# DLRM tower on one core: most of z0's fields move between the k's of the last step's G2

## The chip, the cores and the metric

The kernel runs on one core of one Trainium2 chip. The metric is the device time of one execution in microseconds (us); of the runs the median is given. The engines are TensorE (PE, with its weight loads shown as PEld), VectorE (DVE), ScalarE (ACT), GpSimd (POOL) and SyncE (SP), and each works through its own queue of instructions; semaphores order them among one another.

## The reference

512 samples look up 32 rows of 64 numbers each. Three layers of a compressed interaction network follow, and then a small tower of matrix products:

```
e = stack([tbl_f[ids[:, f]] for f in 32])                     # 512 x 32 x 64
nxt = einsum('bjk,bzk,ojz->bok', h, e, W) + b[:, None]        # three layers, 128 outputs
h, o = nxt[:, :64], nxt[:, 64:]                               # the last layer keeps all of nxt as o
z = sum over k of [o0 | o1 | o2]                              # 512 x 256
h = relu([z | dense_ctx] @ W_top1 + b_top1)
h = relu(h @ W_top2 + b_top2)
y = h @ W_top3
```

All numbers are fp32. Only the sum over k of each layer's o is wanted. Called z0, z1 and z2, these three sums can be had from Gram matrices: z0 is a product of W0 with G0 = e eᵀ of each sample, z1 one of W1 with G1 = h0 eᵀ, z2 one of W2 with G2.

## The kernel before

**Steps.** The samples are taken 16 at a time, in 32 steps. In each step PE computes H (`h_matmuls`, line 383, from products that DVE makes), transposes it (L394), forms G0 (`g0_matmuls`, L403), T (`t_matmuls`, L424 and L427) and G2 (`g2_matmuls`, L440 to L464). T holds, among others, G1 of the step's samples. ACT and DVE copy T from PSUM into T_sb; SP then sends G1 into X and G0 into `kept` by DMA. In the loop G2 of a step stands after H of the next one, and the last step's G2 stands behind the loop.

**Shapes on TensorE.** The 128 by 128 array is used in pieces. A matmul's piece is named in the profile by rows*columns: H and z0 use eight pieces of 32*64, G2, G0 and T four of 64*64, z1 two of 128*64, the transposes of H two of 64*128, z2 and the tower the whole array. An fp32 matmul shows as two passes in the trace, each with its weight load.

**G2.** It runs over k from 0 to 15. Each k has one matmul at L440, one at L444 and two at L450, and from k = 4 on two at L464; the four pieces of the array get 256 columns each.

**The end.** Behind the loop (L505 to L573) PE does z2 of the first half of the samples, six fields of z0, G2 of the last step, five fields of z0, z1, the last five fields of z0, z2 of the second half, and the tower. A field y of z0 is eight matmuls of 128 columns, one for each piece, four into psT and four into psX; all 16 fields add up in the same PSUM banks. The order is written out by hand; there is no scheduler. Before its first matmul G2 waits for the copies of T, and lets SP go on (`t_stored`) to send the last G1; z1 waits for that (`g1_sent`). ACT copies, in this order: G2 (L624), the first half of z2 (L666), z1 (L673), z0's high half (L677), the second half of z2 (L666). DVE adds the two parts of G2 (L810) and the halves of z0 (L840). z2's second half waits for that sum of G2 (`g2_added`), and the tower's first stage (L556) for z0 and z1 (`za_evac`).

Of the kernel before, what the change touches and what calls it, by code (L numbers as in the profile page):

```python
# [19 lines left out]
STEPS = B // SMP  # L20
# [3 lines left out]
HF = NF // 2  # L24
# [24 lines left out]
NTH = [W_SEQUENCE[:k].count(w) for k, w in enumerate(W_SEQUENCE)]  # L49
NSMALL = 9  # L50
NLATE = 6
Z0_CHUNKS = ((0, 6), (6, 11), (11, HF))

T_BY_ACT, T_BY_DVE = (0, 2, 4, 6, 7), (1, 3, 5)
NA, ND = len(T_BY_ACT), len(T_BY_DVE)
# [6 lines left out]
def dlrm_tower(nc, dense_ctx, ids, tables, W_top1, b_top1, W_top2, b_top2, W_top3,  # L62
               W0, b0, W1, b1, W2, b2, y_out):
    ctx = ExitStack()
    with ctx:
# [6 lines left out]
        def sem(name):  # L72
            return ctx.enter_context(nc.semaphore(name))
# [89 lines left out]
        z0_ready, z1_ready, z2_ready = sem("z0_ready"), sem("z1_ready"), sem("z2_ready")  # L163
# [110 lines left out]
        def _(pe):  # L274
# [153 lines left out]
                                  tile_position=(C * h, C))  # L428
                    last.then_inc(t_ready, 1)

            def g2_matmuls(n, first, last_k):
                if first == 0:
                    pe.wait_ge(t_by_act, NA * (n + 1))
                    pe.wait_ge(t_by_dve, ND * (n + 1))
                    pe.sem_inc(t_stored, 1)
                low, high = slice(0, C), slice(C, P)
                cross = T_slots[low, :, :].rearrange("p (v c) s -> p v c s", v=2)[:, :, 0:L_COLS, :]
                for k in range(first, last_k):
                    start, stop = k == 0, k == HF - 1
                    mm(psT[low, 0, 0:HF * SMP], W1d[low, HF + k, :],  # L440
                       cross.rearrange("p v (z y) s -> p v z y s", y=HF)[:, :, :, k, :],
                       start=start, stop=stop, tile_position=(0, 0))
                    row = D_COLS * (k // 8) + HF * (k % 8)
                    mm(psT[high, 0, 0:HF * SMP], W1d[low, k, :], T_flat[low, SMP * row:SMP * (row + HF)],  # L444
                       start=start, stop=stop, tile_position=(0, C))
                    a, i = k // 4, k % 4
                    for v in range(2):
                        out = psT[C * v:C * v + C, 1, 0:HF * SMP]
                        row = D_COLS * v + ROW * i + SHIFT[a]
                        last = mm(out[:, SMP * 4 * a:], W1d[high, HF * v + k, :],  # L450
                                  T_flat[high, SMP * (row + 4 * a):SMP * (row + HF)],
                                  start=start, stop=stop and not a, tile_position=(C, C * v), skip_group_check=True)
                    if a:
                        for v in range(2):
                            out = psT[C * v:C * v + C, 1, 0:HF * SMP]
                            at = D_COLS * v + k
                            rows = T_flat[high, SMP * D_COLS * v:SMP * D_COLS * (v + 1)]\
                                .rearrange("p (i w s) -> p i w s", i=4, s=SMP)
                            if a == 1:
                                moving = rows[:, :, k, :]  # L460
                            else:
                                moving = rows[:, :, k:k + SHIFT[1] * (a - 1) + 1:SHIFT[1], :]\
                                    .rearrange("p i b s -> p b i s")
                            last = mm(out[:, 0:SMP * 4 * a], W1d[high, HF * v + k, :], moving,  # L464
                                      start=False, stop=stop, tile_position=(C, C * v), skip_group_check=True)
                if last_k == HF:
                    last.then_inc(g2_ready, 1)

# [9 lines left out]
            def step(n, lookups):  # L478
                pe.wait_ge(t_by_dve, ND * (n + 1))
                h_matmuls(n + 1)  # L480
                g2_matmuls(n, 0, 4)
                h_transposes(n + 1)
                if lookups:
                    pe.wait_ge(rows_in, 16 * FQ * (n + 1))
                    x_transposes(E_q, psX[:, 3, :])
                g2_matmuls(n, 4, HF)
                if lookups:
                    for evac in x_evac:
                        pe.wait_ge(evac, QUARTERS + n + 1)
                pe.wait_ge(px_ready, n + 2)  # L490
                pe.wait_ge(ht_ready, n + 2)
                tower_in_turn(n + 1)
# [24 lines left out]
                              start=False, stop=(j == 3))  # L517
                last.then_inc(z2_ready, 1)

            def z0(chunk):  # L520
                for y in range(*Z0_CHUNKS[chunk]):
                    for j in range(4):
                        r = slice(Q * j, Q * j + Q)
                        for v in range(2):
                            last = mm(Z0_BANKS[j // 2][C * v:C * v + C, j % 2].rearrange("p (n c) -> p n c", c=4),  # L525
                                      W0z[r, HF * v + y, :], kept[r, :, :, 1 + HF * v + y],
                                      start=(y == 0), stop=(y == HF - 1), tile_position=(Q * j, C * v))
                return last
# [2 lines left out]
            z2(0)  # L531
            pe.wait_ge(t_by_act, NA * STEPS)
            pe.wait_ge(g0_kept, 16 * 4 * STEPS + 1)
            z0(0)
            g2_matmuls(STEPS - 1, 0, HF)
            z0(1)
            pe.wait_ge(g1_sent, 32 * STEPS)
            for y in range(HF):
                for half in range(2):
                    n0 = STEPS // 2 * half  # L540
                    last = mm(psX[C * half:C * half + C, 2, 0:HALF_B].rearrange("p (n s) -> p n s", s=SMP),  # L541
                              W1h[:, y, :], G1_all[:, n0:n0 + STEPS // 2, y, :],
                              start=(y == 0), stop=(y == HF - 1), tile_position=(0, C * half))
            last.then_inc(z1_ready, 1)
            z0(2).then_inc(z0_ready, 1)
            pe.wait_ge(g2_added, 2 + STEPS)
            pe.wait_ge(zb_evac, 1)
            z2(1)
# [14 lines left out]
            for a in range(4):  # L563
                pe.wait_ge(h1_evac, a + 1)
                for m in range(2):
                    last = mm(psX[:, m, :], Wt2[:, a, P * m:P * m + P], h1[:, a, :],
                              start=(a == 0), stop=(a == 3))
                    if a == 3:
                        last.then_inc(h2_ready, 1)
            for a in range(2):  # L570
                pe.wait_ge(h2_evac, a + 1)
                last = mm(psX[0:1, 2, :], Wt3[:, a:a + 1], h2[:, a, :], start=(a == 0), stop=(a == 1))
# [298 lines left out]
```

## Time and profile before

| what | us |
|---|---|
| median of 3 runs | 657.89 (657.76 to 658.94) |
| the profiled execution's own time | 655.34 |
| its span, first to last instruction | 653.6 |
| PE busy in the span | 624.6 |
| DVE, ACT, POOL busy | 483.5, 214.2, 127.9 |
| from z0's first matmul to z2's second half | 603.98 to 626.48 |

The profile shows one execution. Its rows give starts and durations in us, the matmuls' ends are modelled, and several matmuls are in the array at the same time, so that a busy share near 100% says only that PE always had one under way.

### The profile page before, as it was taken

The page shows a single profiled execution, that of the slowest core. Times are in us where ns is not written, and L with a number is a line of the kernel's source. Part 1 is how long each engine was busy: PE and PEld are TensorE (multiplying, and loading weights), DVE is VectorE, ACT ScalarE, POOL GpSimd, SP SyncE. Part 2 cuts the span into 40 slices and gives each one's busy share as a digit, 9 for nine tenths or more (in the row PEclk, how much of TensorE's full clock was granted, in tenths as well). Part 3 has the DMA queues.
Part 4 walks back from the last instruction along what each step waited for, and adds up shares of the span by engine and source line. Part 5 has one row for each costly group of instructions (what it writes and reads, how often), then busy time and mean ns, then how long its engine had stood idle before and what let it go on. Part 6 is the DMA issues. An engine that isn't in the chain of part 4 may idle for free.

```text
span 653.6 us, 32258 instructions
## 1 busy us (share of the span) xinstructions
PE 624.6 (96%) x14488; PEld 516.1 (79%) x14488; DVE 483.5 (74%) x497; ACT 214.2 (33%) x354; POOL 127.9 (20%) x137
## 2 busy tenths in 40 slices
PE   6657999999999999999999999999999999999998
PEld 6645788888888888878888888888888888888773
DVE  4548888888888888878888888888888888841000
ACT  2314333344433433433233333332333333332012
POOL 7764434354445444000000000000000000000000
PEclk9769999999999999999999999999999999999999
DMA  5111111111111111000000000000000000011000
GB/s 183 28 23 31 25 24 26 23 31 28 26 28 29 27 21 28 13 15 13 11 12 11 11 12 11 12 12 12 12 12 12 12 12 12 12 39 45 11 1 0
DMA packets 31659, 14.87 MB, mean 23 GB/s; under 512 B 24178, under 2 KB 28898, under 8 KB 31379
## 3 DMA queue, kind: packets, MB, share of 16 engines
q1 hardware_dynamic: 27442, 10.26, 7.3%
q0 software_dynamic: 4192, 4.25, 2.9%
q8 instruction: 20, 0.33, 0.2%
q14 instruction: 5, 0.03, 0.0%
HBM read 8.03 MB, written 0.00 MB: 12 GB/s over the span
## 4 chain that ended last, share of the span: by engine, by line
PE 91%; POOL 4%; issue 2%; DVE 1%; ACT 1%; DMA 1%; POOLq 0%; DVEq 0%; ACTq 0%
PE psT L440 20%; PE psX L383 20%; PE psT L464 8%; PE psT L424 8%; PE psT L450 7%; PE psT L427 6%; PE psX L424 4%; PE psX L427 4%; POOL G_sb L249 4%; PE psX L394 3%; PE psX L511 2%; PE psX L403 1%; PE psX L283 1%; PE psT L525 1%; PE psX L541 1%
## 5 line engine op out<-in xcount | busy, mean ns | idle before, releaser
L440 PE MATMUL psT<-T_sb,W1d 64*64 64x256 f32 x1024 | 234.3, 379 | 0.0
L444 PE MATMUL psT<-T_sb,W1d 64*64 64x256 f32 x1024 | 234.3, 379 | 0.0
L450 PE MATMUL psT<-T_sb,W1d 64*64 64x256 f32 (+3 forms) x2048 | 205.4, 300 | 0.0
L730 DVE TENSOR_TENSOR prod<-X 128x1024 f32 (+3 forms) x208 | 171.3, 891 | 15.2 <-PE psT L427 14.9
L767 DVE STREAM_TRANSPOSE PT<-prod 128x4608 f32<-128x4608 f32 x31 | 154.0, 4968 | 0.0
L440 PEld LDWEIGHTS psT<-T_sb,W1d 64*64 64x64 f32 x1024 | 131.3, 133 | 27.8 <-issue 14.4
L464 PE MATMUL psT<-T_sb,W1d 64*64 64x64 f32 (+2 forms) x1536 | 141.7, 270 | 0.0
L444 PEld LDWEIGHTS psT<-T_sb,W1d 64*64 64x64 f32 x1024 | 131.4, 133 | 0.0
L383 PE MATMUL psX<-PT,W0T 32*64 32x256 f32 x4464 | 128.5, 377 | 2.6 <-issue 2.4
L383 PEld LDWEIGHTS psX<-PT,W0T 32*64 32x64 f32 x4464 | 113.7, 131 | 20.5 <-issue 18.9
L450 PEld LDWEIGHTS psT<-T_sb,W1d 64*64 64x64 f32 x2048 | 123.6, 133 | 0.8
L185 ACT COPY T_sb<-psT 128x640 f32<-128x640 f32 x160 | 110.2, 709 | 34.4 <-PE psT L427 29.4
L424 PE MATMUL psT<-prod,H_T 64*64 64x288 f32 x640 | 117.1, 407 | 0.4 <-ACT T_sb L185 0.4
L427 PE MATMUL psT<-prod,H_T 64*64 64x320 f32 x640 | 112.9, 434 | 0.0
L264 POOL DMA_INDIRECT E_q<-in_tbl,ids_g x96 | 92.4, 962 | 100.4 <-PE psX L283 67.6
L464 PEld LDWEIGHTS psT<-T_sb,W1d 64*64 64x64 f32 x1536 | 93.2, 134 | 3.4
L185 DVE COPY T_sb<-psX 128x640 f32<-128x640 f32 x93 | 76.7, 825 | 24.0 <-PE psX L427 21.7
L624 ACT COPY G_parts<-psT 128x512 f32<-128x512 f32 x32 | 18.7, 585 | 190.7 <-PE psT L464 190.7
L605 ACT ACTIVATE H_sb<-psX,b_col 128x1024 f32<-128x1024 f32 x32 | 35.7, 1114 | 113.3 <-PE psX L383 109.9
L424 PE MATMUL psX<-prod,H_T 64*64 64x288 f32 x384 | 70.7, 403 | 0.0
L427 PE MATMUL psX<-prod,H_T 64*64 64x320 f32 x384 | 70.4, 429 | 0.0
L424 PEld LDWEIGHTS psT<-prod,H_T 64*64 64x64 f32 x640 | 55.9, 132 | 15.3 <-issue 12.5
(86 smaller groups left out, 551.5 us busy)
## 6 DMA issues: line engine op xcount, KB each, us to landing
X<-T_sb SPq DMA_DIRECT2D x64, 64.0 KB, 2.0
kept<-grams SPq DMA_DIRECT2D x128, 16.5 KB
G_sb<-in_L_rec_W SPq DMA_DIRECT2D x2, 1024.0 KB, 6.6
E_q<-in_tbl,ids_g POOLq DMA_INDIRECT x96
prod<-in_W_top SPq DMA_DIRECT2D x2, 512.0 KB, 3.6
G_sb<-in_L_rec_W SPq DMA_DIRECT2D x1, 512.0 KB, 5.7
G_sb<-in_tbl,ids POOLq DMA_INDIRECT x32, 2.4
dT<-dT SPq DMA_DIRECT2D x3, 32.0 KB
```

Of the source, the lines that this page charges most:

```text
L185: return copy(T_slots[:, :, 2 * t:2 * t + 2], T_BANKS[t][:, :, 0:SLOTS].rearrange("p h c -> p c h"))
L264: nc.gpsimd.indirect_dma_start(out=E_q[:, z - FQ * q, :], out_offset=None, in_=tables[z], in_offset=bass.IndirectOffsetOnAxis(ap=ids_g[:, ...
L383: last = mm(psX[C * v:C * v + C, q, 0:TILES * Q], W0T[r, BLOCKS * v + blk, :], PT_blocks[r, :, BLOCKS * v + blk, :], start=(blk == 0), sto ...
L424: mm(out[0:C].rearrange("p (v c) -> p v c", v=2)[:, :, 0:A_COLS], weights, by_tile[e][r, t, :, D_COLS:D_COLS + A_COLS], start=True, stop=True,
L427: last = mm(out[C:P], weights, by_tile[e][r, t, :, 0:D_COLS], start=True, stop=True, tile_position=(C * h, C))
L440: mm(psT[low, 0, 0:HF * SMP], W1d[low, HF + k, :], cross.rearrange("p v (z y) s -> p v z y s", y=HF)[:, :, :, k, :], start=start, stop=sto ...
L444: mm(psT[high, 0, 0:HF * SMP], W1d[low, k, :], T_flat[low, SMP * row:SMP * (row + HF)], start=start, stop=stop, tile_position=(0, C))
L450: last = mm(out[:, SMP * 4 * a:], W1d[high, HF * v + k, :], T_flat[high, SMP * (row + 4 * a):SMP * (row + HF)], start=start, stop=stop and ...
L464: last = mm(out[:, 0:SMP * 4 * a], W1d[high, HF * v + k, :], moving, start=False, stop=stop, tile_position=(C, C * v), skip_group_check=True)
L605: nc.scalar.activation(H_sb[:, :].rearrange("p (t q r) -> p q t r", t=TILES, r=Q), psX[:, :, 0:TILES * Q].rearrange("p q (t r) -> p q t r" ...
L730: return tt(out, x[:, :, z0:z0 + nz].unsqueeze(3).broadcast_to(shape), x[:, :, y0:y0 + ny].unsqueeze(2).broadcast_to(shape), ALU.mult)
L767: return nc.vector.transpose(PT[:, :].rearrange("p (u c) -> p u c", c=PROD), by_half[e][:, :, 0:PROD])
```

## The change

A field of z0 is no longer bound to three chunks. The first four fields stand ahead of G2. `g2_matmuls` calls a function behind the matmuls of each k, and that function issues one field: field 4 behind k = 0, field 5 behind k = 1, up to field 15 behind k = 11. Behind k = 12 to 14 it issues nothing. z1 follows k = 15, and z2's second half follows z1. `z0_ready` is given by field 15's last matmul. The loop's G2 passes no such function and stays as it was. No matmul, wait, copy or DMA is added or left out.

```diff
-Z0_CHUNKS = ((0, 6), (6, 11), (11, HF))
+
+Z0_ALONE = 4
...
-            def g2_matmuls(n, first, last_k):
+            def g2_matmuls(n, first, last_k, beside=None):
...
+                    if beside and k < HF - 1:
+                        beside(k)
                 if last_k == HF:
                     last.then_inc(g2_ready, 1)
...
-            def z0(chunk):
-                for y in range(*Z0_CHUNKS[chunk]):
+            def z0(first, end):
+                for y in range(first, end):
...
-            z0(0)
-            g2_matmuls(STEPS - 1, 0, HF)
-            z0(1)
+            z0(0, Z0_ALONE)
+
+            def z0_beside(k):
+                if k < HF - Z0_ALONE:
+                    last = z0(Z0_ALONE + k, Z0_ALONE + k + 1)
+                    if k == HF - Z0_ALONE - 1:
+                        last.then_inc(z0_ready, 1)
+
+            g2_matmuls(STEPS - 1, 0, HF, z0_beside)
             pe.wait_ge(g1_sent, 32 * STEPS)
...
             last.then_inc(z1_ready, 1)
-            z0(2).then_inc(z0_ready, 1)
             pe.wait_ge(g2_added, 2 + STEPS)
```

On PE, where the last step's G2 begins, before (W0z marks z0, W1d marks G2; x4 counts matmuls in a row; in brackets what a matmul waits for):

```order
L525 MATMUL psX<-kept,W0z 64x128 x4
L440 MATMUL psT<-T_sb,W1d 64x256 [waits t_by_act,t_by_dve]
L444 MATMUL psT<-T_sb,W1d 64x256
L450 MATMUL psT<-T_sb,W1d 64x256 x2
L440 MATMUL psT<-T_sb,W1d 64x256
```

The same place of PE in the changed kernel, whose lines are 1 to 9 higher:

```order
L528 MATMUL psX<-kept,W0z 64x128 x4
L441 MATMUL psT<-T_sb,W1d 64x256 [waits t_by_act,t_by_dve]
L445 MATMUL psT<-T_sb,W1d 64x256
L451 MATMUL psT<-T_sb,W1d 64x256 x2
L528 MATMUL psT<-kept,W0z 64x128 x4
L528 MATMUL psX<-kept,W0z 64x128 x4
L441 MATMUL psT<-T_sb,W1d 64x256
```

Between the matmuls of k = 0 and those of k = 1 there are now eight of z0; this goes on so up to k = 11.

On PE, from G2's last k to z2's second half, before (W1h marks z1, W2c marks z2; the rows of L525 stand five times in each of the two places):

```order
L464 MATMUL psT<-T_sb,W1d 64x192 x2
L525 MATMUL psT<-kept,W0z 64x128 x4
L525 MATMUL psX<-kept,W0z 64x128 x4
...
L541 MATMUL psX<-X,W1h 64x256 [waits g1_sent]
L541 MATMUL psX<-X,W1h 64x256 x31
L525 MATMUL psT<-kept,W0z 64x128 x4
L525 MATMUL psX<-kept,W0z 64x128 x4
...
L511 MATMUL psX<-G_sb,W2c 128x256 [waits zb_evac,g2_added]
```

The same stretch of PE in the changed kernel:

```order
L451 MATMUL psT<-T_sb,W1d 64x64 x2
L465 MATMUL psT<-T_sb,W1d 64x192 x2
L550 MATMUL psX<-X,W1h 64x256 [waits g1_sent]
L550 MATMUL psX<-X,W1h 64x256 x31
L514 MATMUL psX<-G_sb,W2c 128x256 [waits zb_evac,g2_added]
```

The two runs of five fields are gone from here; z1 touches G2 and z2.

## Rows read from the trace of the kernel before

**Rows 1.** The page: PE's busy time, and the chain by engine.

```profile
PE 624.6 (96%) x14488; PEld 516.1 (79%) x14488; DVE 483.5 (74%) x497; ACT 214.2 (33%) x354; POOL 127.9 (20%) x137
...
PE 91%; POOL 4%; issue 2%; DVE 1%; ACT 1%; DMA 1%; POOLq 0%; DVEq 0%; ACTq 0%
```

**Rows 2.** Stretches: length, busy PE, PEld, DVE, ACT, POOL (instructions), PEclk, DMA.

```profile
545.56:549.63 4.07, 4.07 (x144) 3.65 (x144) 4.03 (x5) 0.60 (x1) 0.00 (x0) 1.00 0.01 2
603.98:607.07 3.09, 3.09 (x98) 2.26 (x97) 0.00 (x0) 0.00 (x0) 0.00 (x0) 1.00 0.00 0
607.07:614.24 7.17, 7.17 (x185) 6.26 (x177) 0.00 (x0) 0.00 (x0) 0.00 (x0) 1.00 0.10 23
614.24:616.83 2.59, 2.59 (x82) 1.82 (x80) 0.43 (x1) 0.96 (x2) 0.00 (x0) 1.00 0.00 0
616.83:623.89 7.06, 7.06 (x73) 4.51 (x65) 0.00 (x0) 0.00 (x0) 0.00 (x0) 1.00 0.01 2
623.89:626.48 2.59, 2.59 (x83) 1.81 (x81) 0.00 (x0) 0.94 (x2) 0.00 (x0) 1.00 0.00 0
626.48:634.57 8.09, 8.09 (x49) 7.12 (x41) 0.75 (x2) 0.83 (x2) 0.00 (x0) 1.00 0.01 2
```

**Rows 3.** Timeline, z0's chunk then G2's start: start, duration, instruction, [idle before].

```profile
606.69 0.45 PE L525 MATMUL psX<-kept,W0z 32*64 32x128 f32 x4
607.07 0.13 PEld L440 LDWEIGHTS psT<-T_sb,W1d 64*64 64x64 f32 x1 [0.44 <-issue]
607.07 0.43 PE L440 MATMUL psT<-T_sb,W1d 64*64 64x256 f32 x1
607.34 0.38 PE L440 MATMUL psT<-T_sb,W1d 64*64 64x256 f32 x1
```

**Rows 4.** Timeline, G2's end, then z0's second chunk with its last pass.

```profile
613.82 0.49 PE L464 MATMUL psT<-T_sb,W1d 64*64 64x192 f32 x3
614.24 0.45 PE L525 MATMUL psT<-kept,W0z 32*64 32x128 f32 x4
...
614.51 0.44 PE L525 MATMUL psX<-kept,W0z 32*64 32x128 f32 x4
...
616.46 0.44 PE L525 MATMUL psX<-kept,W0z 32*64 32x128 f32 x4
```

**Rows 5.** Timeline in the loop: from H to G2.

```profile
549.03 0.67 PE L383 MATMUL psX<-PT,W0T 32*64 32x256 f32 x16
...
549.63 0.43 PE L440 MATMUL psT<-T_sb,W1d 64*64 64x256 f32 x1
```

**Rows 6.** The same iteration: G2 to H's transposes, and back to G2 at k = 4.

```profile
551.21 0.38 PE L450 MATMUL psT<-T_sb,W1d 64*64 64x256 f32 x2
551.52 0.71 PE L394 MATMUL psX<-ident,H_sb 64*128 64x64 f32 x16
552.16 0.43 PE L440 MATMUL psT<-T_sb,W1d 64*64 64x256 f32 x1
...
552.55 0.28 PE L464 MATMUL psT<-T_sb,W1d 64*64 64x64 f32 x4
```

**Rows 7.** Timeline of ACT, DVE and SP around the end.

```profile
595.43 1.30 ACT L185 COPY T_sb<-psT 128x640 f32<-128x640 f32 x2 [0.38 <-PE psT L427]
614.50 0.58 ACT L624 COPY G_parts<-psT 128x512 f32<-128x512 f32 x1 [17.78 <-PE psT L464]
624.01 0.96 ACT L673 ACTIVATE T_sb<-psX,zb 64x256 f32<-64x256 f32 x2 [8.54 <-PE psX L541]
627.03 0.46 ACT L677 ACTIVATE T_sb<-psX,zb 64x256 f32<-64x256 f32 x1
627.57 0.41 DVE L840 TENSOR_TENSOR T_sb<-psX,T_sb 64x256 f32<-64x256 f32 x1
606.32 1.18 SPq L222 DMA_DIRECT2D X<-T_sb  x2
```

**Rows 8.** A stretch of the prologue, columns as in rows 2.

```profile
20.00:40.00 20.00, 9.54 (x136) 7.88 (x134) 7.19 (x16) 5.60 (x16) 15.28 (x16) 0.71 0.12 27
```

## The prediction

> **What bounds the kernel now.** The page comes first: PE has 624.6 of the span's 653.6 us, and the chain of what ended last is PE's for 91% [rows 1]. Second, the stretches of the end: from 603.98 to 634.57 PE is never without work, ACT and DVE are all but idle, and the clock is granted in full [rows 2]. So here the time is what PE takes for its own instructions in their own order, and moving them can only pay or cost inside PE. Third, the timeline at the places where PE passes from one shape of pieces to another, because the change makes many of those.
>
> Within one shape the passes follow closely. G2 goes from its second pass at 607.34 to the second pass of k = 15 at 613.82 in 15 k's [rows 3, 4], 6.48 / 15 = 0.432 us a k. z0 goes from its second pass at 614.51 to its tenth at 616.46 [rows 4], 1.95 / 8 = 0.244 us a pass, 0.487 a field. At a change of shape the next matmul starts just before the last one of the old shape ends: 606.69 + 0.45 = 607.14 against 607.07; 613.82 + 0.49 = 614.31 against 614.24 [rows 3, 4]; in the loop 549.70 against 549.63 and 551.59 against 551.52 [rows 5, 6]. It is 0.07 us ahead of the modelled end each time, whatever the two shapes are, while within a shape two passes overlap by 0.16 us (a pass of G2 lasts 0.38 us and is followed after 0.432 / 2 = 0.216). I read it so: **the old shape's work has to run out before the new shape starts.** The new shape's first weight load begins with its matmul, at 607.07 and not ahead of it, and its first pass takes 0.27 us where the later ones take 0.216 [rows 3].
>
> **The change, part by part.** Call what PE does between two changes of shape a block. Each block takes longer than its passes alone.
>
> - A chunk of five z0 fields takes 2.59 us [rows 2] against 5 x 0.487 = 2.435: 0.155 more. The chunk of six takes 3.09 [rows 2] against 2.92: 0.17 more. The whole G2 takes 7.17 [rows 2] against 16 x 0.432 = 6.91: 0.26 more.
> - A field of z0 alone is a block that no row shows whole, but its two ends are shown: 0.27 from its first pass to its second (614.24 to 614.51) [rows 4], and 0.38 from the second pass to the next shape (606.69 to 607.07) [rows 3]. That is 0.65 against 0.487: 0.163 more.
> - A k of G2 alone, k = 0 to 3: 0.27 from the first pass to the second (607.07 to 607.34) [rows 3] and 0.31 on to the next shape (551.21 to 551.52) [rows 6], 0.58. A k from 4 on also has L464: it starts 0.39 behind the k's first pass (552.16 to 552.55), lasts 0.28, and the next shape would come 0.07 before its end [rows 6], 0.60. The 128- and 192-column forms of later k's give the pieces the same 256 columns, and I take 0.60 for them too. Against 0.432 that is 0.15 to 0.17 more.
>
> The sum. Twelve k's alone: 4 x 0.58 + 8 x 0.60 = 7.12 against 12 x 0.432 = 5.18, **+1.94**. Twelve fields alone: 12 x 0.65 = 7.80 against 5.84, **+1.96**. Gone are the chunks of five and their two surcharges, 2 x 0.155 = **-0.31**. Kept are the surcharge of the first chunk, now of four fields, that of G2's end (k = 12 to 15 stay together) and z1's 7.06 [rows 2]. Together 1.94 + 1.96 - 0.31 = **+3.6 us**. Counted otherwise: five blocks become 27 (four fields; twelve k's; twelve fields; k = 12 to 15; z1), 22 more at 0.16 us.
>
> Nothing covers this and nothing waits anew. G2 starts about two fields, 0.97 us, sooner; the copies of T that it waits for end at 595.43 + 1.30 = 596.73 [rows 7], over 7 us ahead. SP's last sending of G1 goes out with G2's start (606.32) and takes 1.18 us [rows 7]; z1 comes some 17 us behind it. ACT's copy of G2 [rows 7] and the sum behind it have z1's 7.06 us ahead of z2's second half. z1's and z0's copies both fall into that half's 8.09 us: 0.96 for z1, two of about 0.46 for z0 and 0.41 for DVE's last sum [rows 7] make some 2.3 us, so the tower doesn't wait for them. z0 is ready sooner than before, but nobody can use it, since ACT serves z1 first. SP's and POOL's queues are not touched. From z2's second half on everything is later by the same amount.
>
> The profiled execution's own time was 655.34 us with a span of 653.6; with the sum it would be 658.9. The median of the runs shown, 657.89, lies 2.55 us above it; the surcharge is added to the median: 657.89 + 3.6 = **661.5 us**.
>
> The Trainium skill, TensorEngine Tiling (Array Packing), Key Properties, says that changing the tiling mode, and not just the tile, drains the TensorE; by that rule each of the added blocks pays as above, and the trace agrees with its 0.07 us at each of the places read. The Trainium skill, TensorE: Matmul & The Clock Gate, Step-by-step, says of phase 1 that the queue pulls weight loads ahead of running matmuls; across a change of shape the trace doesn't show it (the load at 607.07 starts with its matmul); if it held there, the sum would be rival 1's.
>
> **The rivals.**
>
> 1. *The loads go ahead after all.* If, with work of both shapes dense in the queue, the new weights were loaded ahead, the first pass would take 0.216 instead of 0.27. The 22 added blocks would cost 0.054 less each, 1.2 us: +2.4, 660.3 us. Against it stands the load at 607.07, and that z0 was queued without a break behind G2 at 614.24 as well, with a first pass of 0.27 [rows 3, 4]. Chance 0.05. That is also what the rule of the Trainium skill's page TensorE: Matmul & The Clock Gate, Step-by-step, on loads ahead of matmuls would give.
> 2. *Shapes share the array (the other side: not slower).* H's passes, in the same pieces as z0's, take 4.07 / 18 = 0.226 us for 256 columns [rows 2], z0's 0.244 for 128. So columns don't bound a z0 pass; about half of it, 0.12, could be filled by G2's. If a field and a k ran into one another so, each of the twelve pairs would gain 2 x 0.12, and the two chunks' surcharges would go: -2.9 - 0.3 = -3.2, 654.7 us. It decides from the point at which a block's surcharge falls below nothing. Against it: z0's passes use all eight pieces, so each lies over G2's four, and in the loop, too, no start of another shape lies earlier than 0.07 ahead of the end [rows 5, 6]. Chance 0.04.
> 3. *A k alone costs as the whole of G2.* Where L464 comes late, the end of G2 costs more: 0.26 over its passes. If each of the eight k's from 4 on paid 0.26 instead of 0.168, +0.74: 662.2 us. The row of k = 4 speaks against it [rows 6]. Chance 0.05.
> 4. *The clock falls.* In the prologue, with PE at work for 9.54 of 20 us, the granted clock was 0.71 on the mean [rows 8], so part of it at 1.2 GHz. The interleaved stretch (7.12 + 7.80 = 14.9 us) leaves the array partly empty; at 1.2 GHz throughout it would add up to 14.9 us, 676 us. But the loop's stretch with H has changes of shape too and keeps 1.00 [rows 2], and no gap between modelled ends and starts opens. Chance 0.02.
>
> **How the numbers follow.** The forecast has 0.84 and predicts 661.5 us. The range takes in rivals 1 and 3. Its lower end is 660.3 less 0.3 for the median of another series, 660.0; its upper end is 662.2 and 1.0 more, since one of three runs lay 1.05 above the median: 663.2. Outside are rivals 2 and 4 and a little of the rest. About 0.2%, 1.3 us, is what a measurement of this kernel can tell from no change. The forecast and rivals 1, 3 and 4 are slower by more than that; 0.03 of them are lost to the spread of the runs. So slower 0.93, the same 0.03, faster 0.04.
>
> **What would show it.** In the profile of the changed kernel the stretch from z0's first matmul to z2's second half should take 22.5 + 3.6 = 26.1 us. In it a k and a field should take 1.24 us together, twelve times over, with each change of shape 0.07 us ahead of the modelled end before it; the clock stays at 1.00, and the stretch from z2's second half to the end keeps its length. I'm wrong if a k and a field take about 0.92 us or less (the shapes overlap, or a change is free), if one of the shapes' first passes takes 0.22 us (rival 1), or if PE waits at z1 or at z2's second half.

## The result and the profile after

The changed kernel takes 660.55 us (median of 13 runs, 658.06 to 662.88), the kernel before 657.26 us in the same number of runs (656.18 to 658.94). The ratio is 1.005 with a 95% interval of 1.0037 to 1.0064: **slower by 3.3 us**, between 2.4 and 4.2 by the interval. The forecast was 661.5 us, +3.6 us.

The profiled execution took 660.56 us with a span of 658.9 us. These are the stretches of its end, each block or group of blocks by itself, with the columns of [rows 2]: length, then busy time (instructions) of PE, PEld, DVE, ACT and POOL, the granted clock, DMA share and GB/s.

```profile
605.73:607.83 2.10, 2.10 (x65) 1.42 (x64) 0.00 (x0) 0.00 (x0) 0.00 (x0) 1.00 0.00 0
607.83:622.74 14.91, 14.91 (x328) 7.28 (x320) 0.00 (x0) 0.00 (x0) 0.00 (x0) 1.00 0.05 12
622.74:624.67 1.93, 1.93 (x56) 1.65 (x48) 0.00 (x0) 0.00 (x0) 0.00 (x0) 1.00 0.00 0
624.67:631.73 7.06, 7.06 (x68) 4.48 (x65) 0.42 (x1) 0.96 (x2) 0.00 (x0) 1.00 0.01 2
631.73:639.82 8.09, 8.09 (x42) 7.12 (x40) 0.75 (x2) 1.77 (x4) 0.00 (x0) 1.00 0.00 0
605.73:631.73 26.00, 26.00 (x497) 14.83 (x497) 0.42 (x1) 0.96 (x2) 0.00 (x0) 1.00 0.03 8
```

The rows are the four fields ahead of G2, the twelve k's with a field behind each, k = 12 to 15, z1, z2's second half, and the whole from z0's first matmul to z2's second half. That whole is 26.00 us where [rows 2] add up to 22.50: **+3.50 us**. PE is busy in every stretch, the clock is granted in full, and PE's busy share would tell nothing of the loss.

The timeline of PE shows where it lies. One field, one k and the start of the next field, the starts and durations in us:

```profile
609.66 0.45 PE L528 MATMUL psT<-kept,W0z 32*64 32x128 f32 x4
...
609.91 0.44 PE L528 MATMUL psT<-kept,W0z 32*64 32x128 f32 x4
609.94 0.44 PE L528 MATMUL psX<-kept,W0z 32*64 32x128 f32 x4
610.31 0.13 PEld L441 LDWEIGHTS psT<-T_sb,W1d 64*64 64x64 f32 x1 [0.41 <-issue]
610.31 0.43 PE L441 MATMUL psT<-T_sb,W1d 64*64 64x256 f32 x1
...
610.58 0.38 PE L441 MATMUL psT<-T_sb,W1d 64*64 64x256 f32 x1
...
610.59 0.38 PE L451 MATMUL psT<-T_sb,W1d 64*64 64x256 f32 x2
...
610.90 0.45 PE L528 MATMUL psT<-kept,W0z 32*64 32x128 f32 x4
```

A field takes 0.65 us (609.66 to 610.31) and a k 0.59 (610.31 to 610.90). Each change of shape comes 0.07 us ahead of the modelled end of the last matmul (609.94 + 0.44 = 610.38 against 610.31; 610.59 + 0.38 = 610.97 against 610.90), as at every place in [rows 3 to 6], and the first weight load of the new shape starts with its matmul.

**The span has grown by more, 5.3 us.** z0 starts at 605.73, where before it was 603.98; the 1.75 us between lie ahead of the changed instructions. From z2's second half to the end both have 27.13 us. ACT's first copy of H at L605 (L613 in the changed kernel) already comes 2.00 us later, so the difference arises ahead of that copy; first the kernel before, then the changed one:

```profile
69.36 1.11 ACT L605 ACTIVATE H_sb<-psX,b_col 128x1024 f32<-128x1024 f32 x1 [3.29 <-PE psX L383]
```

```profile
71.36 1.11 ACT L613 ACTIVATE H_sb<-psX,b_col 128x1024 f32<-128x1024 f32 x1 [4.80 <-PE psX L384]
```

In the prologue's stretch of [rows 8] this execution was granted less clock, 0.64 on the mean against 0.71. That this made the difference is not shown: the interleaved run with one shape (below) was granted 0.79 there, and its z0 starts later still, at 608.23. The changed kernel's row, then that run's:

```profile
20.00:40.00 20.00, 9.44 (x134) 7.78 (x132) 6.77 (x17) 5.59 (x16) 15.13 (x16) 0.64 0.12 27
```

```profile
20.00:40.00 20.00, 7.59 (x138) 6.30 (x136) 6.94 (x17) 5.68 (x17) 15.16 (x16) 0.79 0.14 27
```

In the eleven profiles of this study z0 starts anywhere from 603.98 to 608.33 us, and the order of the work ahead of it is the same in all of them. So one execution's total can't tell 3 us, and below the stretch from z0's first matmul to z2's second half is compared. Its parts repeat to hundredths of a us from kernel to kernel (z1 takes 7.06, a whole G2 in one block 7.17). Each stretch is from one profile, and of the experiments only the layout alone and the layout with one run of fields have more than one timed execution.

### The profile page after: what moved, and what is told of

It is laid out like the page before. It is cut to its first block, busy times and chain, and to the rows that moved or that the text cites. A ratio compares the mean times of both kernels' runs of the same rounds, so it can differ in the third digit from the quotient of the medians.

```text
span 658.9 us, 32258 instructions
## 1 busy us (share of the span) xinstructions
PE 628.9 (95%) x14488; PEld 514.3 (78%) x14488; DVE 483.5 (73%) x497; ACT 214.2 (33%) x354; POOL 128.0 (19%) x137
## 4 chain that ended last, share of the span: by engine, by line
PE 91%; POOL 4%; issue 2%; DVE 1%; ACT 1%; DMA 1%; POOLq 0%; DVEq 0%; ACTq 0%
PE psT L441 20%; PE psX L384 20%; PE psT L465 8%; PE psT L425 7%; PE psT L451 7%; PE psT L428 6%; PE psX L425 4%; PE psX L428 4%; POOL G_sb L250 4%; PE psX L395 3%; PE psX L514 2%; PE psX L404 1%; PE psT L528 1%; PE psX L284 1%; PE psX L550 1%
## 5 line engine op out<-in xcount | busy, mean ns | idle before, releaser
L445 PE MATMUL psT<-T_sb,W1d 64*64 64x256 f32 x1024 | 236.8, 380 | 0.0
L441 PE MATMUL psT<-T_sb,W1d 64*64 64x256 f32 x1024 | 236.8, 380 | 0.0
L465 PE MATMUL psT<-T_sb,W1d 64*64 64x64 f32 (+2 forms) x1536 | 141.7, 270 | 0.0
L465 PEld LDWEIGHTS psT<-T_sb,W1d 64*64 64x64 f32 x1536 | 93.2, 134 | 3.4
L613 ACT ACTIVATE H_sb<-psX,b_col 128x1024 f32<-128x1024 f32 x32 | 35.7, 1114 | 114.8 <-PE psX L384 111.4
```

The lines of the kernel that those rows point to most:

```text
L441: mm(psT[low, 0, 0:HF * SMP], W1d[low, HF + k, :], cross.rearrange("p v (z y) s -> p v z y s", y=HF)[:, :, :, k, :], start=start, stop=sto ...
L613: nc.scalar.activation(H_sb[:, :].rearrange("p (t q r) -> p q t r", t=TILES, r=Q), psX[:, :, 0:TILES * Q].rearrange("p q (t r) -> p q t r" ...
```

## The experiments

The theory is that each added block between two changes of shape pays about 0.16 us. The first rival is that interleaving as such slows both kinds of matmuls, whatever their shapes.

### Half as many blocks

```diff
-                if k < HF - Z0_ALONE:
-                    last = z0(Z0_ALONE + k, Z0_ALONE + k + 1)
+                if k < HF - Z0_ALONE and k % 2 == 1:
+                    last = z0(Z0_ALONE + k - 1, Z0_ALONE + k + 1)
```

> Two fields of z0 stand behind every second k up to k = 11, so there are 15 blocks between changes of shape where the kernel before has 5 and the changed one 27. The measure is the stretch from z0's first matmul to z2's second half, 22.50 us before and 26.00 us in the changed kernel. Theory (each added block pays about 0.16 us for the change of shape, whatever it holds): 22.50 + 10 x 0.16 = 24.1 us. Rival (it is the interleaving of every field with every k as such, alternating operands and PSUM banks, that slows both kinds of matmuls in proportion): all twelve fields and twelve k's are still interleaved, so it stays near 26.0 us.

```profile
605.17:629.26 24.09, 24.09 (x497) 15.95 (x497) 0.43 (x1) 0.96 (x2) 0.00 (x0) 1.00 0.04 8
```

24.09 us, as the theory has it: every field still stands among the k's, and more than half of the loss is gone.

### Fewer blocks than before

```diff
-Z0_CHUNKS = ((0, 6), (6, 11), (11, HF))
+Z0_CHUNKS = ((0, HF),)
...
-            z0(0)
+            z0(0).then_inc(z0_ready, 1)
             g2_matmuls(STEPS - 1, 0, HF)
-            z0(1)
...
-            z0(2).then_inc(z0_ready, 1)
```

> All 16 fields of z0 stand in one run ahead of G2, then G2, z1 and z2: 3 blocks instead of 5. Theory: 22.50 - 2 x 0.155 = 22.19 us for the stretch from z0's first matmul to z2's second half, a gain that the total time can't show but the trace can. Rival (chunks of z0 between others are free or help): 22.50 us or more.

```profile
605.25:613.20 7.95, 7.95 (x257) 6.47 (x256) 0.00 (x0) 0.00 (x0) 0.00 (x0) 1.00 0.01 2
613.20:620.37 7.17, 7.17 (x184) 6.26 (x176) 0.00 (x0) 0.00 (x0) 0.00 (x0) 1.00 0.10 23
620.37:627.43 7.06, 7.06 (x66) 4.51 (x65) 0.42 (x1) 0.96 (x2) 0.00 (x0) 1.00 0.01 2
```

z0, G2 and z1 take 22.18 us; 22.19 were expected. The four orders lie on a line: 3, 5, 15 and 27 blocks take 22.18, 22.50, 24.09 and 26.00 us, 0.16 us a block.

### The same order without a change of shape

Both runs give z0's matmuls 64 rows, so that z0 and G2 use the same pieces; the first has the order of the changed kernel, the second that of the kernel before.

```diff
-                        r = slice(Q * j, Q * j + Q)
+                        r = slice(C * (j // 2), C * (j // 2) + C)
...
-                                      start=(y == 0), stop=(y == HF - 1), tile_position=(Q * j, C * v))
+                                      start=(y == 0), stop=(y == HF - 1), tile_position=(C * (j // 2), C * v))
```

> The changed kernel's order, but z0's matmuls take 64 rows instead of 32, so that their pieces are 64*64 as G2's (z0 sums over rows that don't belong to it, so its numbers are not z0's; count, columns and operands' sizes stay). Theory (the cost is the change of shape): against the same pieces in the order of the kernel before, the 24 passages between G2 and z0 cost nothing, and two passages to and from z1 go, so this stretch is 0.1 to 0.4 us shorter than that of the other run with 64 rows, and passages overlap as passes within a shape do. Rival (interleaving itself): it is longer than the other by about 3.5 us.

> The order of the kernel before, with z0's matmuls over 64 rows in pieces of 64*64 as in the run before (z0's numbers are not z0's). It is the base of that run. A field has four matmuls of 128 columns for each of two row halves, two to a piece. If a pass is bound by what each piece can take (0.24 us), a field takes 4 x 0.24 = 0.97 us, 0.48 more than before; if by the columns streamed (0.107), 0.43. Theory: between z0 and G2 there is no jump of 0.31 to 0.38 us in the starts, while to and from z1 there still is.

The whole stretch, interleaved and in chunks:

```profile
608.23:638.01 29.78, 29.78 (x497) 25.19 (x496) 0.43 (x1) 0.96 (x2) 0.00 (x0) 1.00 0.03 7
```

```profile
606.44:636.38 29.94, 29.94 (x497) 23.69 (x496) 0.43 (x1) 1.90 (x4) 0.00 (x0) 1.00 0.03 6
```

Interleaved it is 0.16 us shorter, not 3.5 us longer; it has one block less, two against three, since no fields follow z1. The timeline of the interleaved run shows passages that overlap:

```profile
612.58 0.41 PE L528 MATMUL psT<-kept,W0z 64*64 64x128 f32 x2
...
613.33 0.43 PE L528 MATMUL psX<-kept,W0z 64*64 64x128 f32 x2
613.52 0.40 PE L441 MATMUL psT<-T_sb,W1d 64*64 64x256 f32 x1
...
613.81 0.39 PE L451 MATMUL psT<-T_sb,W1d 64*64 64x256 f32 x2
613.98 0.41 PE L528 MATMUL psT<-kept,W0z 64*64 64x128 f32 x2
```

G2 starts 0.24 us before the modelled end of z0's last pass, and z0 0.22 us before that of G2's. With the shape the same, interleaving costs nothing; it is **the change of shape** that costs. Nor does it gain: a field and the k behind it take 1.40 us (612.58 to 613.98), which is a field's 0.97 and a k's 0.43 added up. The larger pieces are no way out: a field has twice as many passes to a piece and takes 0.97 us (in chunks, the six ahead of G2 take 5.84, from 606.44 to G2's first start at 612.28).

### What bounds a pass of z0

The second rival of the prediction rested on a z0 pass not being bound by its columns. This run asks by what.

```diff
+            kept_flat = kept[:, :, :, :].rearrange("p n q f -> p (n q f)")
+
...
-                            last = mm(Z0_BANKS[j // 2][C * v:C * v + C, j % 2].rearrange("p (n c) -> p n c", c=4),
-                                      W0z[r, HF * v + y, :], kept[r, :, :, 1 + HF * v + y],
+                            last = mm(Z0_BANKS[j // 2][C * v:C * v + C, j % 2],
+                                      W0z[r, HF * v + y, :], kept_flat[r, P * y:P * y + P],
```

The output goes to the same 128 places as before; it is only no longer described in groups of four.

> The order of the kernel before, but each z0 matmul streams 128 numbers that lie side by side in each partition of kept, where the real ones lie 34 numbers apart (so z0's numbers are not z0's). It asks what bounds a z0 pass, 0.244 us for 128 columns where H's passes in the same pieces take 0.22 for 256. If the distance of the numbers read bounds it, a pass falls to between 0.107 (128 columns) and 0.22 us, and the 16 fields' 32 passes save 0.8 to 4.4 us of the 22.50 us from z0's first matmul to z2's second half. If the weight loads or the issue of eight matmuls bound it, it stays at 0.244 and the stretch at 22.5 us. The surcharge at changes of shape stays at 0.16 us a block in either case.

The first chunk of six fields, where [rows 2] have 3.09 us, the second of five, where they have 2.59, and the whole stretch:

```profile
606.17:607.75 1.58, 1.58 (x97) 1.41 (x97) 0.00 (x0) 0.00 (x0) 0.00 (x0) 1.00 0.00 0
...
614.92:616.28 1.36, 1.36 (x82) 1.19 (x81) 0.42 (x1) 0.96 (x2) 0.00 (x0) 1.00 0.00 0
...
606.17:624.70 18.53, 18.53 (x497) 14.56 (x497) 0.42 (x1) 1.90 (x4) 0.00 (x0) 1.00 0.04 10
```

A field more costs 1.58 - 1.36 = 0.22 us, two passes of 0.11 and not of 0.244. The stretch fell to 18.53 us, 3.97 less. It was the distance of the numbers that z0 streams, not the weight loads and not the number of matmuls. The expected surcharge of 0.16 us a block was a miss here: the chunk of five takes 1.36 - 5 x 0.22 = 0.26 over its passes.

### A layout that keeps z0's numbers together

The chunks' order is that of the kernel before; only the last two dimensions of `grams` and `kept` are exchanged, in the copies, the DMA and the matmuls that use them.

```diff
-        grams = sb("grams", [P, 4, GRAM])
+        grams = sb("grams", [P, GRAM, 4])
-        kept = sb("kept", [P, STEPS, 4, NS])
+        kept = sb("kept", [P, STEPS, NS, 4])
...
-                                      W0z[r, HF * v + y, :], kept[r, :, :, 1 + HF * v + y],
+                                      W0z[r, HF * v + y, :], kept[r, :, 1 + HF * v + y, :],
```

> The order of the kernel before; kept and grams hold the four numbers of a field side by side (16 bytes), where before the fields lay side by side and the four numbers 136 bytes apart. Every number computed is the same. If a z0 pass is bound by single numbers far apart, runs of four are read faster: a pass between 0.109 us (as with all 128 side by side) and 0.244, the stretch from z0's first matmul to z2's second half between 18.5 and 22.5 us, and the total up to 4.0 us shorter than before (ratio down to 0.994). If only wholly adjacent numbers are fast, the stretch stays at 22.5 us and the ratio at 1.000.

```profile
608.33:626.86 18.53, 18.53 (x497) 14.56 (x497) 0.42 (x1) 1.90 (x4) 0.00 (x0) 1.00 0.04 10
```

```profile
608.33 0.34 PE L525 MATMUL psT<-kept,W0z 32*64 32x128 f32 x4
...
608.49 0.29 PE L525 MATMUL psT<-kept,W0z 32*64 32x128 f32 x4
...
608.60 0.29 PE L525 MATMUL psT<-kept,W0z 32*64 32x128 f32 x4
```

Four numbers side by side are as good as 128: passes at 608.49 and 608.60, 0.11 us apart, and 18.53 us for the stretch. The median is 654.12 us against 657.49 for the kernel before in the same comparison, a ratio of 0.9943 (0.9918 to 0.9968): **this version beats both kernels**, the one before by 3.4 us (2.1 to 5.4 by the interval) and with it the changed one, which was slower than that. The output is described in groups of four again, as in the kernel before, so it is the reading of `kept` that counts. z2's second half, which streams `kept` as well, takes 7.94 us where [rows 2] have 8.09:

```profile
626.86:634.80 7.94, 7.94 (x45) 7.04 (x40) 0.75 (x2) 0.83 (x2) 0.00 (x0) 1.00 0.01 2
```

The total holds more than these stretches: with the layout the DMAs of the whole kernel need 19370 packets instead of 31659, and what that is worth was not measured by itself. ACT pays for the layout: its copy of `grams` takes 0.66 us on the mean where it took 0.39. That is off PE's path, since in both profiles the copies of H in the loop come 16.87 us apart (median).

### The layout with fewer and with more blocks

The first run puts all 16 fields ahead of G2, as above; the second has the order of the changed kernel.

> The same layout, and all 16 fields of z0 in one run ahead of G2 (3 blocks instead of 5). The run with adjacent numbers showed chunks of z0 that take 0.27 us more than their passes of 0.109, so two chunks fewer save 0.54 us against the layout alone, if its passes are that short, and 0.31 us if they stay at 0.244. Best case 18.0 us for the stretch and 4.5 us less in total than before (ratio 0.993). Rival (fewer blocks don't help): the stretch of the layout alone.

> The same layout in the order of the changed kernel. If every added block costs the same 0.16 us whatever its passes take, this stretch is 3.5 us longer than that of the layout alone. If a block's cost is a fixed time from its last pass to the next shape, less what a pass would have taken anyway, blocks of short passes pay more: 12 k's at 0.16, 12 fields at 0.27, less two chunks at 0.27, together +4.6 us.

The first is a miss: 19.23 us, longer than the layout alone, and a ratio of 0.9951 (0.9926 to 0.9976) to the kernel before, not to be told from 0.9943. Its timeline where G2 begins:

```profile
610.36 0.43 PE L440 MATMUL psT<-T_sb,W1d 64*64 64x256 f32 x1
611.55 0.13 PEld L440 LDWEIGHTS psT<-T_sb,W1d 64*64 64x64 f32 x1 [1.07 <-issue]
611.55 0.43 PE L440 MATMUL psT<-T_sb,W1d 64*64 64x256 f32 x1 [0.77 <-issue]
```

After one pass of L440 PE stands still for 0.77 us, and "issue" says that it waits for nothing that the profile shows. The z0 run ahead of it went as expected (606.55 to 610.36, 3.81 us). From the second start of L440 to z1, G2 takes the 7.17 us of a whole G2 elsewhere:

```profile
611.55:618.72 7.17, 7.17 (x176) 6.23 (x176) 0.00 (x0) 0.00 (x0) 0.00 (x0) 1.00 0.06 15
```

So the miss lies in the 1.19 us between the two starts of L440; without it the stretch would be, by an estimate from these rows, 3.81 + 7.17 + 7.06 = 18.04 us, close to the best case.

The interleaved layout takes 22.13 us, 3.60 more than the layout alone. That is near the 3.5 us of a fixed price a block and not the 4.6 us that I set against it:

```profile
604.35:626.48 22.13, 22.13 (x497) 14.37 (x496) 0.42 (x1) 0.96 (x2) 0.00 (x0) 1.00 0.04 9
```

```profile
608.08 0.34 PE L528 MATMUL psT<-kept,W0z 32*64 32x128 f32 x4
...
608.48 0.43 PE L441 MATMUL psT<-T_sb,W1d 64*64 64x256 f32 x1
```

A short field alone takes 0.40 us (608.08 to 608.48), 0.40 - 0.22 = 0.18 over its passes. The 0.27 that I had taken from the chunks and put on every single field was wrong for those. Why a run of five short fields pays 0.26 to 0.27 and one field 0.18 is not shown.

### Two runs of fields, with the layout

```diff
-Z0_CHUNKS = ((0, 6), (6, 11), (11, HF))
+Z0_CHUNKS = ((0, 6), (6, HF))
```

> The layout with the four numbers of a field side by side, z0 in two runs: six fields ahead of G2, ten behind it, then z1 and z2: 4 blocks where the layout alone has 5. In the run with all 16 fields ahead of G2 PE stood still for 0.77 us between the two passes of G2's first k, with nothing that the profile shows to wait for, and the next 16 KB of instructions had come in only 0.2 us before that k. If fewer blocks pay and that standstill came from instructions not yet there behind a long run of short matmuls, this stretch is 18.53 - 0.27 = 18.26 us, or shows a standstill of its own behind the ten fields. If fewer blocks don't pay with this layout, it is 18.5 us without one.

18.60 us, with a standstill in the middle of the ten fields:

```profile
605.80:624.40 18.60, 18.59 (x497) 14.54 (x496) 0.42 (x1) 0.96 (x2) 0.00 (x0) 1.00 0.05 11
```

```profile
616.15 0.28 PE L525 MATMUL psX<-kept,W0z 32*64 32x128 f32 x2
616.44 0.34 PE L525 MATMUL psT<-kept,W0z 32*64 32x128 f32 x4
```

No start for 0.29 us, and the next passes begin as they do behind a change of shape, though none is there. So a long run of short passes gives back what one block fewer saves. That instructions come too late would fit both standstills, but no run shows it. In this one no fetch of instructions falls into the standstill (616.15 to 616.44): the DMA queue of instructions has the nearest at 613.8 and 617.5. Nor was the fetch in the run with all 16 fields ahead of G2 as close as the expectation says: it lies at 609.2, 1.1 us and not 0.2 ahead of G2's first start at 610.36. The cause is open.

## Why the prediction was right

- **What bounds.** PE alone, in its own order, at full clock: held. Every stretch after has PE busy throughout, and the part behind z2's second half kept its 27.13 us.
- **A field alone**, put together from two places of the trace, 0.65 us: measured 0.65. **A k alone**, 0.58 and 0.60: measured 0.59 and, from k = 4 on, 0.60 (612.79 to 613.39 for k = 4). Twelve of both were to take 7.12 + 7.80 = 14.92 us; they took 14.91.

```profile
612.79 0.43 PE L441 MATMUL psT<-T_sb,W1d 64*64 64x256 f32 x1
...
613.39 0.45 PE L528 MATMUL psT<-kept,W0z 32*64 32x128 f32 x4
```

- **The surcharges gone and kept.** Two chunks' worth gone, z1 unchanged at 7.06: held. G2's end was expected to keep 0.26 us over its passes, 1.99 us for k = 12 to 15; it took 1.93. That is most of the difference between +3.6 and +3.50. This one term was a little too large: in the kernel before, z0 follows 0.42 us behind G2's last pass (613.82 to 614.24 [rows 4]); here z1 follows 0.36 behind it (624.31 to 624.67), and the last matmuls of the late kind (L464, here L465) take 0.33 and not 0.49.

```profile
624.31 0.38 PE L441 MATMUL psT<-T_sb,W1d 64*64 64x256 f32 x1
...
624.41 0.33 PE L465 MATMUL psT<-T_sb,W1d 64*64 64x192 f32 x2
624.67 0.44 PE L550 MATMUL psX<-X,W1h 128*64 128x256 f32 x2
```

- **Nothing waits anew.** The order on ACT and DVE moved inside z2's second half, as said. z1's copies start at 631.85, z0's follow, and DVE's last sum ends at 633.75 + 0.41 = 634.16, 5.7 us ahead of the tower's first stage at 639.82:

```profile
631.85 0.96 ACT L681 ACTIVATE T_sb<-psX,zb 64x256 f32<-64x256 f32 x2 [5.93 <-PE psX L550]
...
633.21 0.46 ACT L685 ACTIVATE T_sb<-psX,zb 64x256 f32<-64x256 f32 x1
```

```profile
633.75 0.41 DVE L848 TENSOR_TENSOR T_sb<-psX,T_sb 64x256 f32<-64x256 f32 x1
```

- **Rival 1, loads ahead.** Fell: the first weight load at 610.31 starts with its matmul, and G2's first pass takes 0.27 (610.31 to 610.58). The prediction had this rival's price too high. Its 0.27 for z0's first pass runs from psT's start to psX's; from psT to psT it is 0.25 (609.66 to 609.91), next to 0.244 for the later ones. So loads ahead could have saved 0.054 only at the twelve k's, 0.65 us and not 1.2. z0's surcharge lies behind its last pass: 0.40 to the next shape (609.91 to 610.31) instead of 0.244. The Trainium skill, TensorE: Matmul & The Clock Gate, Step-by-step, tells of weight loads pulled ahead of running matmuls; at these changes of shape the trace doesn't show it.
- **Rival 2, shapes share the array.** Fell: no start lies earlier than 0.07 us ahead of the old shape's end. Its premise was half right. That columns don't bound a z0 pass held, and the layout shows how to get at that time. That G2's passes could fill it was not borne out even within one shape, where passes do run into one another: a field and a k take 1.40 us there, their 0.97 and 0.43 added up.
- **Rivals 3 and 4.** No k cost 0.26 us over its passes, and the clock stayed at 1.00.
- **The median.** +3.3 us, where the stretch gives +3.5; the interval, +2.4 to +4.2 us, holds both. Of the 0.95 us between 661.5 and 660.55, 0.6 is the kernel before, which came out that much lower in 13 runs than in the first three.

The Trainium skill, TensorEngine Tiling (Array Packing), Key Properties, has the rule for this case: a change of tiling mode drains TensorE, a change of tile alone doesn't. The runs agree with both halves: interleaving two shapes took 3.50 us more, interleaving one shape 0.16 us less. The price here was 0.16 us for each block between two changes.

## What to carry to other kernels

In these runs matmuls of different piece shapes didn't fill one another's gaps on TensorE. Count the changes of shape in an order, price them from the trace (last start of the old shape to first start of the new one, less a pass, and what the new shape's first pass takes more than its later ones), and put work of one shape together. Where a pass takes longer than its columns (here 0.244 us for 128 where another line streams 256 in 0.22), look first at how the streamed numbers lie in memory: that was worth 4 us of this stretch, where fewer blocks gave 0.3.

## What the runs showed beyond the expectation

- Streamed numbers that lie 136 bytes apart take 0.244 us for 128 columns, in fours side by side (16 bytes) 0.11 us, the same as all 128 side by side. The Trainium skill, SBUF — State Buffer, Door 1: The DMA port swizzle (the note on cachelines there), says that reads within a 16-byte line run at full bandwidth and reads that go to a new line each time pay. The runs agree: four fp32 numbers side by side are as fast as 128, and single ones take a bit more than double the time. No run has two or three side by side, so the length of a line is not shown.
- With short passes a run of 16 fields was followed by a standstill of 0.77 us, and a run of ten had one of 0.29 in it, with nothing in the profile that PE waited for. Each was seen in one profile.
- z0's start differs by up to 4.4 us between the profiles (603.98 to 608.33), which is more than the whole effect of the change. Most of it is there at ACT's first copy of H at that line (69.36 to 73.59). The clock granted from 20 to 40 us doesn't put these starts in order (0.71 at 603.98, 0.79 at 608.23), so the cause is open.
